# A graph layer on one core: q and k as two more columns of the value projection, denominators behind the weights

## The chip, the cores and the metric

One Trainium2 chip, one of its cores. The metric is device microseconds of one execution of the whole kernel, median of several runs. The kernel is written by hand: each engine has its own program, and engines wait for each other through semaphores.

## The reference

The input x is 32 batches of 512 channels by 1024 nodes, float32. What is computed per batch:

```
h = max(layernorm(x over the nodes), 0)
q = wq . h ; k = wk . h                     (one number per node)
scores[m, n] = leaky(q[n] + k[m])           (slope 0.01)
att = softmax(scores over n)
agg[c, m] = sum_n h[c, n] att[m, n]
out = x + max(adj . agg + bm, 0)            (adj is 512 x 512)
```

## The kernel before

The kernel multiplies the weights in first: v = h^T adj^T (1024 nodes by 512 outputs, `v_tile`), then out = v^T att (`unit`). Every product of two float32 operands is made of three f16 matmuls, hi.hi, hi.lo and lo.hi, so all tiles exist as an upper and a lower part (`h_hi`, `h_lo`, `v_hi`, `v_lo`, `p_hi`, `p_lo`).

**TensorE.** The work of one batch b is a period: eight units of 24 matmuls, each 512 columns wide (L385 to L387; units 0 to 3 are the first half of the output nodes, 4 to 7 the second), and then the v phase of batch b+2: eight node tiles of 12 matmuls, 512 columns (L362 to L364). In front of the v phase stands `project_qk`: 32 matmuls of 256 columns that fill the array four at a time with the small wq/wk tile (L325). Behind tile 1 stands `select_qk` (L334), which brings q and k to one column per node; behind tile 3 `spread_qmax` (L340). In unit 5 of each batch, ahead of node tile 2, stands `transpose_ab` (L347), which turns the scales of the next batch's softmax into rows. The accumulators are four PSUM banks `mix`, used in turn; a v tile takes one.

**The softmax.** leaky(q + k) splits: exp of it is the larger of two products of a row factor and a column factor. `exponentials` (ScalarE) makes the factors `cols` from `logs` (`q_head`, `q_tail` on VectorE). SyncE writes two of them to DRAM and loads them spread over all partitions as `den_row` (`write_den_rows`, `load_den_rows`). `denominator` (VectorE, L728) makes the row sums, 16 instructions a batch; `row_scales` (L735 to L739) their reciprocals. After `transpose_ab` and `copy_ab` (L685), SyncE writes and loads them as `ab_row`. The weights themselves are made in 16 steps a batch, eight for each half: `leak` (ScalarE, L491) into one of three PSUM banks `ring`, `weight` (VectorE, L749), `p_upper` (ScalarE, L499), `p_lower` (VectorE, L756).

**VectorE** runs `early(b)`: half 1 of batch b, whose eight weights are each followed by two denominators of batch b+1, then `row_scales`, two `h_lower`, `copy_ab`, two `h_lower`; and `late(b)`: half 0 of batch b+1, then the eight `v_lower` (L761) of batch b+2 with `q_rows`, `q_head`, `q_tail`, the `statistics` (L633) and the `normaliser` (L649 to L662, a chain of small dependent operations) of batch b+3 between them.

**ScalarE** runs in step: leak and p_upper, the normalised tiles `h_upper` (L465) and `h_full` (L471), `relu` of each unit (L512), `v_upper` (L503). **GpSimd** adds the residual to each unit (`finish`, L911). **SyncE** issues all transfers in one order: stores, residual loads, the ab rows, x of batch b+3, and at the end of the period the denominator rows of batch b+2.

Who waits for what around the change, as before has it:

```
            def transpose_ab(b):
                if at(b, first):
                    pe.wait_ge(s_az, 1)
                    pe.wait_ge(s_qc, Q_OPS + 4)
                pe.wait_ge(s_dn, cnt(b, D_OPS, D_OPS))
```

The first two batches are taken apart in a prologue of its own, written out by hand.

Of the kernel before, what the change touches and what calls it, by code (L numbers as in the profile page):

```python
# [25 lines left out]
F32 = mybir.dt.float32  # L26
F16 = mybir.dt.float16
# [16 lines left out]
def gnn_layer(nc, x, adj, wq, wk, bm, out):  # L44
# [7 lines left out]
    QG = 32  # L52
    NQ = P // QG
    QN = N // NQ
# [4 lines left out]
    with ExitStack() as ctx:  # L59
# [23 lines left out]
        wmT_hi = sb("wmT_hi", [P, CT, O], F16)  # L83
        wmT_lo = sb("wmT_lo", [P, CT, O], F16)
        wm_nat = sb("wm_nat", [P, OT, C])
        wqk = sb("wqk", [P, CT, QG], F16)
        select = sb("select", [P, NQ, 2])
        qk_rows = sb("qk_rows", [P, QN])
# [21 lines left out]
        ln_shift = sb("ln_shift", [P, 2, CT])  # L110
        qk = sb("qk", [P, 2, NT])
# [14 lines left out]
        mix = [bank(f"mix{i}") for i in range(MIX)]  # L126
# [3 lines left out]
        assert CT == 4 and NT == 8  # L130
        assert QN == 2 * P and NT == 2 * NQ
        rows_ps = small[:, 0:QN]
        ab_ps = small[:, 0:P]
        qk_ps = small[:, QN:QN + 2 * NT].rearrange("p (c g i) -> p c g i", c=2, i=2)
# [12 lines left out]
        s_wz = sem("wqk_zeroed")  # L147
        s_un = sem("unscales_ready")
        s_sel = sem("select_ready")
        s_wqk = sem("wqk_ready")  # L150
        s_wm = sem("wm_scaled")
# [8 lines left out]
        s_qk = sem("qk_done")  # L160
# [52 lines left out]
        def _(sp):  # L213
# [55 lines left out]
            write_den_rows(second)  # L269
            load_den_rows(second)  # L270

            def period(b, one, two, three):
                store(b, 0)
# [12 lines left out]
                if two:  # L286
                    write_den_rows(nxt(b, 2))
                    load_den_rows(nxt(b, 2))

# [14 lines left out]
        def _(pe):  # L304
            def transposed_weights():
                pe.wait_ge(s_id, 2)
                for ot in range(OT):
                    pe.wait_ge(s_wm, ot + 1)
# [6 lines left out]
            def project_qk(b):  # L315

                pe.wait_ge(s_hlo, cnt(b, CT, CT))
                if at(b, second):
                    pe.wait_ge(s_qc, 4)
                else:  # L320
                    wait(pe, s_at, cnt(b, 1, 0))
                for ct in range(CT):
                    for part, hp in enumerate((h_hi, h_lo)):
                        for g in range(NQ):
                            mm = pe.matmul(rows_ps[g * QG:(g + 1) * QG, :], wqk[:, ct, :],  # L325
                                           hp[:, b[1], ct, g * QN:(g + 1) * QN],
                                           start=(ct == 0 and part == 0), stop=(ct == CT - 1 and part == 1),
                                           tile_position=(0, g * QG))
                mm.then_inc(s_qk, 1)

            def select_qk(b):
                pe.wait_ge(s_qc, cnt(b, Q_OPS, 1))
                for c in range(2):
                    mm = pe.matmul(qk_ps[:, c, :, :], qk_rows[:, c * P:(c + 1) * P], select[:, :, :],  # L334
                                   start=True, stop=True)
                mm.then_inc(s_qk, 1)
# [5 lines left out]
            def transpose_ab(b):  # L342
                if at(b, first):
                    pe.wait_ge(s_az, 1)
                    pe.wait_ge(s_qc, Q_OPS + 4)
# [3 lines left out]
            def v_tile(b, nt):  # L349

                if nt < MIX and at(b, second):
                    pe.wait_ge(s_vlo[nt % 2], (nt + MIX) // 2 + 1)
                elif nt < MIX:
                    wait(pe, s_y[nt % 2], cnt(b, U // 2, (nt + MIX) // 2 + 1 - U))
                else:
                    pe.wait_ge(s_vlo[nt % 2], cnt(b, NT // 2, (nt - MIX) // 2 + 1))
                ps, nodes = mix[nt % MIX], slice(nt * P, (nt + 1) * P)
                for ct in range(CT):
                    if nt == 0 and at(b, first):
                        pe.wait_ge(s_wl, ct + 1)  # L360
# [585 lines left out]
```

## Time and profile before

| | us |
|---|---|
| median of 3 runs | 2088.57 |
| lowest and highest | 2087.33, 2088.61 |
| the profiled execution | 2090.47 |
| its span, first to last instruction | 2088.7 |
| TensorE busy (share of the span) | 2051.5 (98%) |
| VectorE busy | 1674.8 (80%) |
| ScalarE busy | 1221.5 (58%) |
| GpSimd busy | 379.6 (18%) |

Busy time counts an instruction from its start to its end; matmuls overlap, so their durations (379 ns for one of 512 columns) are longer than the step from one start to the next. The chain of waits that ended last lies on TensorE for 95% of the span.

### The profile page before, as it was taken

How to read it: one execution, taken by the hardware profiler on the slowest of the kernel's cores; microseconds unless marked ns; L12 is line 12 of the kernel's file. 1: busy time of each engine (PE TensorE's matmuls, PEld its weight loads, DVE VectorE, ACT ScalarE, POOL GpSimd, SP SyncE). 2: the span in 40 equal slices, each digit the busy share in tenths (PEclk: the TensorE clock that was granted, in tenths of full speed). 3: DMA queues.
4: the chain of work that ended last, by engine and by line, in shares of the span. 5: the costliest groups of instructions: out<-in, count | busy, mean ns of one | idle time of the engine just before them, and what ended most of it. 6: DMA issues, size and time to landing. Idle time of an engine off the chain costs nothing.

```text
span 2088.7 us, 33534 instructions
## 1 busy us (share of the span) xinstructions
PE 2051.5 (98%) x10448; PEld 950.3 (45%) x10448; DVE 1674.8 (80%) x3661; ACT 1221.5 (58%) x1871; POOL 379.6 (18%) x273
## 2 busy tenths in 40 slices
PE   5899999999999999999999999999999999999999
PEld 2344444444444444444444444444444444444444
DVE  7978878778887788887788877888877888778853
ACT  5556656556655566565566555665655665556634
POOL 1012211112111122111121111221111211112212
PEclk9999999999999999999999999999999999999999
DMA  5244433344324444333433234442334432343332
GB/s 195 64 155 142 148 99 123 138 160 141 133 84 136 151 141 146 104 118 137 161 141 133 84 136 151 141 146 105 117 137 161 141 131 86 136 152 141 106 101 76
DMA packets 126395, 271.46 MB, mean 130 GB/s; under 512 B 22624, under 2 KB 23136, under 8 KB 122208
## 3 DMA queue, kind: packets, MB, share of 16 engines
q1 hardware_dynamic: 123904, 269.01, 37.1%
q10 hardware_dynamic: 2400, 1.58, 0.3%
q14 instruction: 76, 0.62, 0.1%
q8 instruction: 15, 0.25, 0.1%
HBM read 202.91 MB, written 67.63 MB: 130 GB/s over the span
## 4 chain that ended last, share of the span: by engine, by line
PE 95%; DVE 3%; DMA 1%; POOL 0%; issue 0%; ACT 0%; POOLq 0%; SPq 0%; DVEq 0%
PE mix L385 21%; PE mix L387 21%; PE mix L386 21%; PE mix L362 10%; PE mix L363 10%; PE mix L364 10%; PE small L325 2%; DVE den_out L728 1%; PE small L334 1%; DMA xs<-in_x_dram 0%; DVE p_ring L749 0%; DVE p_lo L756 0%; DVE v_lo L761 0%; POOL wm_nat L893 0%; DMA den_row<-den_rows 0%
## 5 line engine op out<-in xcount | busy, mean ns | idle before, releaser
L385 PE MATMUL mix<-p_hi,v_hi 128*128 128x512 f16 x2048 | 776.3, 379 | 5.9 <-DVE p_lo L756 5.4
L386 PE MATMUL mix<-p_lo,v_hi 128*128 128x512 f16 x2048 | 776.2, 379 | 0.0
L387 PE MATMUL mix<-p_hi,v_lo 128*128 128x512 f16 x2048 | 776.2, 379 | 0.0
L911 POOL TENSOR_TENSOR res<-res,y 128x512 f32<-128x512 f32 x256 | 370.5, 1447 | 1688.2 <-ACT y L512 1688.2
L749 DVE SCALAR_TENSOR_TENSOR p_ring<-ab_row,cols,p_ring 128x512 f32<-128x512 f32 x512 | 377.1, 748 | 129.7 <-ACT p_ring L491 129.7
L491 ACT ACTIVATE p_ring<-ab_row,cols 128x512 f32<-128x512 f32 x512 | 349.5, 691 | 192.4 <-DMA ab_row<-ab_rows 132.3
L503 ACT ACTIVATE v_hi<-mix 128x512 f16<-128x512 f32 x256 | 152.7, 597 | 444.1 <-PE mix L364 443.5
L728 DVE SCALAR_TENSOR_TENSOR den_out<-den_row,cols 128x512 f32<-128x512 f32 x512 | 393.4, 806 | 1.0 <-DMA den_row<-den_rows 1.0
L362 PE MATMUL mix<-wmT_hi,h_hi 128*128 128x512 f16 x1024 | 389.1, 380 | 0.0
L364 PE MATMUL mix<-wmT_hi,h_lo 128*128 128x512 f16 x1024 | 388.8, 380 | 0.0
L363 PE MATMUL mix<-wmT_lo,h_hi 128*128 128x512 f16 x1024 | 388.8, 380 | 0.0
L756 DVE SCALAR_TENSOR_TENSOR p_lo<-p_ring,p_hi 128x512 f16<-128x512 f32 x512 | 351.6, 687 | 19.3 <-ACT p_hi L499 14.9
L499 ACT ACTIVATE p_hi<-p_ring 128x512 f16<-128x512 f32 x512 | 303.0, 592 | 67.8 <-DVE p_ring L749 67.5
L761 DVE SCALAR_TENSOR_TENSOR v_lo<-mix,v_hi 128x512 f16<-128x512 f32 x256 | 176.7, 691 | 195.6 <-ACT v_hi L503 191.7
L385 PEld LDWEIGHTS mix<-p_hi,v_hi 128*128 128x128 f16 x2048 | 200.3, 98 | 249.7 <-DVE p_lo L756 8.5
L387 PEld LDWEIGHTS mix<-p_hi,v_lo 128*128 128x128 f16 x2048 | 200.4, 98 | 241.6
L386 PEld LDWEIGHTS mix<-p_lo,v_hi 128*128 128x128 f16 x2048 | 200.4, 98 | 237.2
L512 ACT ACTIVATE y<-mix,bias_o,unscale_o 128x512 f32<-128x512 f32 x256 | 195.8, 765 | 29.2 <-PE mix L387 29.2
L471 ACT ACTIVATE h<-xs,ln_shift,ln_scale 128x1024 f32<-128x1024 f32 x120 | 145.0, 1232 | 107.3 <-DVE h_lo L691 107.3
L633 DVE BATCH_NORM_STATS2 stats<-xs 128x6 f32<-128x512 f32 x248 | 158.3, 680 | 8.6 <-DMA xs<-in_x_dram 8.6
L362 PEld LDWEIGHTS mix<-wmT_hi,h_hi 128*128 128x128 f16 x1024 | 103.0, 101 | 119.2 <-issue 5.9
L364 PEld LDWEIGHTS mix<-wmT_hi,h_lo 128*128 128x128 f16 x1024 | 100.3, 98 | 121.4 <-issue 1.0
(71 smaller groups left out, 838.9 us busy)
## 6 DMA issues: line engine op xcount, KB each, us to landing
res<-in_x_dram SPq DMA_DIRECT2D x256, 256.0 KB, 3.2
out_dram<-res SPq DMA_DIRECT2D x256, 256.0 KB, 2.1
xs<-in_x_dram SPq DMA_DIRECT2D x124, 512.0 KB, 6.5
den_row<-den_rows SPq DMA_DIRECT2D x32, 1024.0 KB, 4.6
ab_row<-ab_rows SPq DMA_DIRECT2D x64, 512.0 KB, 5.0
res<-in_x_dram SPq DMA_DIRECT2D x4, 512.0 KB, 5.0
wm_nat<-in_adj_dram ACTq DMA_DIRECT2D x1, 1024.0 KB, 12.2
den_rows<-cols SPq DMA_DIRECT2D x32, 8.0 KB, 1.6
```

The source lines that it names most:

```text
L362: pe.matmul(ps[:, :], hi, wmT_hi[:, ct, :], start=(ct == 0), stop=False)
L363: pe.matmul(ps[:, :], hi, wmT_lo[:, ct, :], start=False, stop=False)
L364: mm = pe.matmul(ps[:, :], lo, wmT_hi[:, ct, :], start=False, stop=(ct == CT - 1))
L385: pe.matmul(ps[:, :], v_hi[:, b[1], nt, chans], p_hi[:, hf, nt, :], start=(nt == 0), stop=False)
L386: pe.matmul(ps[:, :], v_hi[:, b[1], nt, chans], p_lo[:, hf, nt, :], start=False, stop=False)
L387: mm = pe.matmul(ps[:, :], v_lo[:, b[1], nt, chans], p_hi[:, hf, nt, :], start=False, stop=(nt == NT - 1))
L491: act.activation(ring[t % RING][:, :], ab_row[:, 1, hf * HALF:(hf + 1) * HALF], ACT.Copy, scale=cols[:, b[1], 1, nt:nt + 1]).then_inc(s_lk, 1)
L499: act.activation(p_hi[:, hf, nt, :], ring[t % RING][:, :], ACT.Copy, scale=P_SCALE).then_inc(s_phi, 1)
L728: dve.scalar_tensor_tensor(out=den_out[:, nodes], in0=den_row[:, 0, nodes], scalar=cols[:, b[1], 2, nt:nt + 1], in1=den_row[:, 1, nodes], ...
L749: dve.scalar_tensor_tensor(out=ring[t % RING][:, :], in0=ab_row[:, 0, hf * HALF:(hf + 1) * HALF], scalar=cols[:, b[1], 0, nt:nt + 1], in1= ...
L756: dve.scalar_tensor_tensor(out=p_lo[:, hf, nt, :], in0=ring[t % RING][:, :], scalar=P_SCALE, in1=p_hi[:, hf, nt, :], op0=ALU.mult, op1=ALU ...
L911: pool.tensor_tensor(res[:, k, :], res[:, k, :], y[:, k % 2, :], ALU.add).then_inc(s_add, 1)
```

## The change

q and k are no longer projected apart. The tiles `wmT_hi` and `wmT_lo` are cut into two halves of 256 outputs, and the first half has two more columns, wq and wk. A v tile takes two PSUM banks (`pair`), half a bank each, and each of its 12 matmuls of 512 columns becomes one of 258 and one of 256. So there are two v tiles' worth of accumulators in place of four, and a tile waits for the split of the tile two before it. ScalarE copies the two columns out ahead of `v_hi`, as `qk4`. `project_qk` and `select_qk` go, but the first batch keeps a projection of its own of 96 matmuls with two columns.

`q_head` of batch b+1 moves to the start of `early(b)`, `q_tail` behind the third p_lo of half 1, `exponentials` behind the fourth p_hi, and SyncE's denominator rows to the start of its period. All 16 denominators stand behind the weights of half 1. `transpose_ab` stands ahead of node tile 0 of unit 5, `spread_qmax` in unit 0 ahead of node tile 6. On ScalarE the normalised tiles move behind half 1, between the relus; relu 7 moves into half 0. The normaliser moves from behind v_lower 6 to behind v_lower 5.

```diff
             def v_tile(b, nt):
+                if nt == 0:
+                    pe.wait_ge(s_hlo, cnt(b, CT, CT))
...
-                ps, nodes = mix[nt % MIX], slice(nt * P, (nt + 1) * P)
+                    pe.wait_ge(s_vlo[nt % 2], cnt(b, NT // 2, nt // 2))
+                ps, nodes = pair[nt % 2], slice(nt * P, (nt + 1) * P)
...
-                    pe.matmul(ps[:, :], hi, wmT_hi[:, ct, :], start=(ct == 0), stop=False)
-                    pe.matmul(ps[:, :], hi, wmT_lo[:, ct, :], start=False, stop=False)
-                    mm = pe.matmul(ps[:, :], lo, wmT_hi[:, ct, :], start=False, stop=(ct == CT - 1))
+                    for half, cols_of in enumerate((OH + QK, OH)):
+                        pe.matmul(ps[:, half, 0:cols_of], hi, wmT_hi[:, ct, half, 0:cols_of],
+                                  start=(ct == 0), stop=False)
+                    for half, cols_of in enumerate((OH + QK, OH)):
+                        pe.matmul(ps[:, half, 0:cols_of], hi, wmT_lo[:, ct, half, 0:cols_of], start=False, stop=False)
+                    for half, cols_of in enumerate((OH + QK, OH)):
+                        mm = pe.matmul(ps[:, half, 0:cols_of], lo, wmT_hi[:, ct, half, 0:cols_of],
+                                       start=False, stop=(ct == CT - 1))
                 mm.then_inc(s_v, 1)
...
                 for nt in range(NT):
-                    if one and k == MIX + 1 and nt == 2:
+                    if one and k == MIX + 1 and nt == 0:
                         transpose_ab(nxt(b))
+                    if one and (k, nt) == ((1, 2) if at(b, first) else (0, 6)):
+                        spread_qmax(nxt(b))
...
             def early(b, one, two):
                 h = nxt(b, 2)
+                if one:
+                    q_head(nxt(b))
                 weight(b, NT)
                 for nt in range(NT):
                     if nt < NT - 1:
                         weight(b, NT + nt + 1)
-                    if one:
+                    p_lower(b, NT + nt)
+                    if one and nt == 2:
+                        q_tail(nxt(b))
+                if one:
+                    for nt in range(NT):
                         denominator(nxt(b), nt)
-                    p_lower(b, NT + nt)
-                if one:
                     row_scales(nxt(b))
...
@@ ScalarE, period @@
-                    if two and nt in (0, 3, 7):
-                        h_upper(h, (0, 3, 7).index(nt))
-                    if two and nt in (1, 5):
-                        h_full(h, nt // 4)
-                    if nt in (2, 4, 6):
-                        relu(b, nt // 2 - 1)
+                    if one and nt == 3:
+                        exponentials(nxt(b))
+                    if nt == 5:
+                        relu(b, 0)
                 if two:
+                    h_upper(h, 0)
+                    h_full(h, 0)
+                relu(b, 1)
+                if two:
+                    h_upper(h, 1)
+                    h_full(h, 1)
+                relu(b, 2)
+                if two:
+                    h_upper(h, 2)
                     h_upper(h, 3)
                 relu(b, 3)
```

The prologue changes too: VectorE scales half of the projection weights, GpSimd the other half and wq and wk, and the hand-written orders of both are new.

How the instructions move, VectorE, `early` of one batch, from the last step but one of half 1 to the first transfer's source (L749 is `weight`, L728 `denominator`, L756 `p_lower`, L735 to L739 `row_scales`, L691 `h_lower`, L685 `copy_ab`); before:

```order
L749 SCALAR_TENSOR_TENSOR p_ring<-ab_row,cols,p_ring 128x512
L728 SCALAR_TENSOR_TENSOR den_out,den_part<-den_row,cols 128x512 x2
L756 SCALAR_TENSOR_TENSOR p_lo<-p_ring,p_hi 128x512
L728 SCALAR_TENSOR_TENSOR den_out,den_part<-den_row,cols 128x512 x2
L756 SCALAR_TENSOR_TENSOR p_lo<-p_ring,p_hi 128x512
L735 TENSOR_TENSOR den<-den_part 128x8
L737 RECIPROCAL ab_pad<-den 128x8
L739 TENSOR_TENSOR ab_pad<-cols,ab_pad 128x8
L691 TENSOR_TENSOR h_lo<-h,h_hi 128x1024 x2
L685 COPY ab_t<-small 16x128
```

and in the changed kernel (L729 weight, L736 p_lower, L708 denominator, L715 to L719 row_scales, L670 h_lower, L664 copy_ab):

```order
L729 SCALAR_TENSOR_TENSOR p_ring<-ab_row,cols,p_ring 128x512
L736 SCALAR_TENSOR_TENSOR p_lo<-p_ring,p_hi 128x512 x2
L708 SCALAR_TENSOR_TENSOR den_out,den_part<-den_row,cols 128x512 x16
L715 TENSOR_TENSOR den<-den_part 128x8
L717 RECIPROCAL ab_pad<-den 128x8
L719 TENSOR_TENSOR ab_pad<-cols,ab_pad 128x8
L670 TENSOR_TENSOR h_lo<-h,h_hi 128x1024 x2
L664 COPY ab_t<-small 16x128
```

The denominators are now 16 in one run.

SyncE, the denominator rows and the stores around them; before (L237 and L241 are the denominator rows out and in, L232 a store, L228 a residual load; the period of the first batch begins with the first store below, and the rows ahead of it are the second batch's):

```order
L252 DMA ab_row<-ab_rows 128x2x512 x2
L237 DMA den_rows<-cols 128x2x8
L241 DMA den_row<-den_rows 128x2048
L232 DMA out_dram<-res 128x512 x2
L228 DMA res<-in_x_dram 128x512
```

and in the changed kernel, from the end of the first period into the second:

```order
L224 DMA res<-in_x_dram 128x512 x2
L233 DMA den_rows<-cols 128x2x8
L237 DMA den_row<-den_rows 128x2048
L228 DMA out_dram<-res 128x512 x2
L224 DMA res<-in_x_dram 128x512
```

The transfers L233 and L237 read alike, but in the changed kernel they are of the next batch, whose exponentials are made in half 1 of this period; before they were of the batch after the next, made in the v phase.

## Rows read from the trace of the kernel before

**Rows 1.** the page: busy time of TensorE (PE), its weight loads (PEld) and the others.

```profile
PE 2051.5 (98%) x10448; PEld 950.3 (45%) x10448; DVE 1674.8 (80%) x3661; ACT 1221.5 (58%) x1871; POOL 379.6 (18%) x273
```

**Rows 2.** timeline of TensorE, one period: start us, us, engine, line, instruction.

```profile
979.53 0.38 PE L385 MATMUL mix<-p_hi,v_hi 128*128 128x512 f16 x1
...
1006.72 0.27 PE L347 MATMUL small<-ident,ab_pad 128*128 128x128 f32 x1
1006.83 0.38 PE L385 MATMUL mix<-p_hi,v_hi 128*128 128x512 f16 x1
...
1020.86 0.38 PE L387 MATMUL mix<-p_hi,v_lo 128*128 128x512 f16 x1
...
1022.16 0.39 PE L362 MATMUL mix<-wmT_hi,h_hi 128*128 128x512 f16 x1
...
1027.13 0.38 PE L364 MATMUL mix<-wmT_hi,h_lo 128*128 128x512 f16 x1
...
1027.71 0.38 PE L362 MATMUL mix<-wmT_hi,h_hi 128*128 128x512 f16 x1
```

**Rows 3.** timeline of VectorE (DVE), same period.

```profile
978.39 0.20 DVE L649 BATCH_NORM_AGGREGATE moments<-stats 128x2 f32<-128x12 f32 x1
...
981.32 0.69 DVE L761 SCALAR_TENSOR_TENSOR v_lo<-mix,v_hi 128x512 f16<-128x512 f32 x1
...
998.85 1.76 DVE L728 SCALAR_TENSOR_TENSOR den_out<-den_row,cols 128x512 f32<-128x512 f32 x1
...
1000.54 0.74 DVE L728 SCALAR_TENSOR_TENSOR den_out<-den_row,cols 128x512 f32<-128x512 f32 x1
...
1001.21 0.68 DVE L756 SCALAR_TENSOR_TENSOR p_lo<-p_ring,p_hi 128x512 f16<-128x512 f32 x1
...
1003.76 0.62 DVE L735 TENSOR_TENSOR den<-den_part 128x8 f32<-128x8 f32 x1
...
1004.82 2.36 DVE L691 TENSOR_TENSOR h_lo<-h,h_hi 128x1024 f16<-128x1024 f32 x2
...
1013.67 1.42 DVE L749 SCALAR_TENSOR_TENSOR p_ring<-ab_row,cols,p_ring 128x512 f32<-128x512 f32 x2 [3.88 <-ACT p_ring L491]
...
1024.63 0.41 DVE L700 COPY qk_rows<-small 128x256 f32<-128x256 f32 x1
1025.59 0.69 DVE L761 SCALAR_TENSOR_TENSOR v_lo<-mix,v_hi 128x512 f16<-128x512 f32 x1 [0.55 <-ACT v_hi L503]
...
1034.33 0.28 DVE L712 TENSOR_REDUCE qmax<-small 128x1 f32<-128x128 f32 x1
...
1035.05 1.28 DVE L633 BATCH_NORM_STATS2 stats<-xs 128x6 f32<-128x512 f32 x2
```

**Rows 4.** timeline of ScalarE (ACT), the first exponential.

```profile
1036.28 0.21 ACT L480 ACTIVATE cols<-logs 128x16 f32<-128x16 f32 x1
```

**Rows 5.** timeline of SyncE's queue, the load of the denominator rows.

```profile
1038.09 0.33 SPq L241 DMA_DIRECT2D den_row<-den_rows  x1
```

**Rows 6.** that load (L241), all 32 of them, from issue to landing.

```profile
DMA to landing us min/median/max: 4.2/4.6/5.3
```

**Rows 7.** timeline of GpSimd (POOL), same period.

```profile
994.64 1.55 POOL L911 TENSOR_TENSOR res<-res,y 128x512 f32<-128x512 f32 x1 [3.65 <-ACT y L512]
998.79 1.27 POOL L911 TENSOR_TENSOR res<-res,y 128x512 f32<-128x512 f32 x1 [2.60 <-ACT y L512]
1002.64 1.71 POOL L911 TENSOR_TENSOR res<-res,y 128x512 f32<-128x512 f32 x1 [2.58 <-ACT y L512]
```

**Rows 8.** the page's costliest groups: ScalarE's relu and full tile, busy, mean ns.

```profile
L512 ACT ACTIVATE y<-mix,bias_o,unscale_o 128x512 f32<-128x512 f32 x256 | 195.8, 765 | 29.2 <-PE mix L387 29.2
L471 ACT ACTIVATE h<-xs,ln_shift,ln_scale 128x1024 f32<-128x1024 f32 x120 | 145.0, 1232 | 107.3 <-DVE h_lo L691 107.3
```

**Rows 9.** timeline of TensorE, prologue, the first v tile.

```profile
30.40 0.59 PE L362 MATMUL mix<-wmT_hi,h_hi 128*128 128x512 f16 x1
```

**Rows 10.** timeline of VectorE, prologue, the first weight.

```profile
75.81 1.42 DVE L749 SCALAR_TENSOR_TENSOR p_ring<-ab_row,cols,p_ring 128x512 f32<-128x512 f32 x2 [0.76 <-ACT p_ring L491]
```

More of the change, by code:

```diff
@@ L123, in gnn_layer @@
         ab_dram = nc.dram_tensor("ab_rows", (2, NT, P), F32, kind="Internal").ap()
-        mix = [bank(f"mix{i}") for i in range(MIX)]
+        pair = [ctx.enter_context(nc.psum_tensor(f"pair{i}", [P, 2, 512], F32)) for i in range(2)]
+        mix = [pair[i // 2][:, i % 2, :] for i in range(MIX)]
         ring = [bank(f"p_ring{i}") for i in range(RING)]
@@ L313, in transposed_weights, with project_first_qk @@
                             mm.then_inc(s_wt, 1)
[L315 to L335, printed above, removed]
+            def project_first_qk():
+                pe.wait_ge(s_wqk, 2)
+                pe.wait_ge(s_hlo, CT)
+                for nt in range(NT):
+                    for ct in range(CT):
+                        nodes = slice(nt * P, (nt + 1) * P)
+                        hi, lo = h_hi[:, 0, ct, nodes], h_lo[:, 0, ct, nodes]
+                        w_hi, w_lo = wmT_hi[:, ct, 0, OH:], wmT_lo[:, ct, 0, OH:]
+                        pe.matmul(qk_ps[:, nt, :], hi, w_hi, start=(ct == 0), stop=False)
+                        pe.matmul(qk_ps[:, nt, :], hi, w_lo, start=False, stop=False)
+                        mm = pe.matmul(qk_ps[:, nt, :], lo, w_hi, start=False, stop=(ct == CT - 1))
                 mm.then_inc(s_qk, 1)
@@ L502, in v_upper @@
                 act.wait_ge(s_v, cnt(b, NT, nt + 1))
[L503 removed]
+                ps = pair[nt % 2]
+                if not at(b, first):
+                    act.activation(qk4[:, nt, :], ps[:, 0, OH:OH + QK], ACT.Copy)
+                act.activation(v_hi[:, b[1], nt, :].rearrange("p (h o) -> p h o", h=2), ps[:, :, 0:OH], ACT.Copy,
                                scale=1.0 / H_SCALE).then_inc(s_vhi, 1)
@@ L575, in _ @@
             v_upper(second, 2)
-            exponentials(second)
             v_upper(second, 3)
@@ L835, in _ @@
             denominator(first, 0)
-            for ct in range(CT):
-                h_lower(second, ct)
-                v_lower(first, 3 + ct)
-                denominator(first, 1 + ct)
+            h_lower(second, 0)
+            v_lower(first, 3)
+            denominator(first, 1)
+            h_lower(second, 1)
+            v_lower(first, 4)
+            h_lower(second, 2)
+            v_lower(first, 5)
+            denominator(first, 2)
+            h_lower(second, 3)
+            v_lower(first, 6)
+            denominator(first, 3)
             v_lower(first, 7)
-            q_rows(second)
+            denominator(first, 4)
             denominator(first, 5)
+            v_lower(second, 0)
             denominator(first, 6)
-            q_head(second)
             denominator(first, 7)
             row_scales(first)
-            q_tail(second)
-            v_lower(second, 0)
             v_lower(second, 1)
```

185 lines of the change are left out of this document (73 added, 112 removed).

## The prediction

> **What bounds the kernel now.** I read the page's busy times first. TensorE is busy 98% of the span, and it has as many weight loads as matmuls [rows 1], so the second use of one stationary tile loads it again. Then I read one period of TensorE's timeline, from the first matmul of a batch's unit 0 at 979.53, which I call time zero; times written +x below are us from there [rows 2]. From 1006.83 to 1020.86 are 65 matmuls of 512 columns with no hole, 0.2158 us each: 213.3 ns of columns at the upper clock level of 2.4 GHz, and 2.5 ns beside them. The period is 288 of these (62.16), two transposes of 0.11, and the q and k part: from the last matmul before it to the first tile is 1.30, less one step 1.08; the select is 0.58 less 0.2158, so 0.36 [rows 2]. Sum 63.8. Nothing waits: everything else is cover. Next I read VectorE (DVE), because it decides when TensorE could be made to wait. Its reciprocal chain ends at 1004.82, which is +25.3, and TensorE asks for it at 1006.72, which is +27.2 [rows 2, 3]. That margin of 1.9 us is the number to watch.
>
> **What comes off TensorE.** 1.08 + 0.36 = 1.44 us a period. Spread and transpose stay.
>
> **What goes on.** Every 512-column matmul becomes 258 and 256 columns. By columns at 2.4 GHz and 2.5 ns each, that is 110.0 + 109.2 = 219.2 ns for 215.8. Times 96 it is +0.32 us a period. Lower bound 0.08 (only the two columns more). Upper bound: if a load were not covered by a matmul half as long, it costs about what the select's load and 8-column matmul cost, 0.36/4 = 0.09 us each, 17 us a period. I take the low value, as a 128x128 f16 load already lies under the transpose, whose step is 0.11 [rows 2]. The Trainium skill (TensorE: Matmul & The Clock Gate, LDWEIGHTS) gives columns / 1.2 ns for a load, 107 ns here, so it would be covered with 2 ns to spare; no run here shows such loads in a row. Net on TensorE: -1.1 us a period, 30 periods with a v phase, -33 us.
>
> **The two-bank tiles.** A tile may now start only when the tile two before it is split, where it was four. v_lo starts 0.84 after a tile's end (1022.16 + 12 x 0.2158 = 1024.75, then 1025.59) and takes 0.69 [rows 2, 3]. The qk4 copy adds 0.1 to 0.2 on ScalarE (a small operation there is 0.21 [rows 4]). Done 1.7 after the tile's end, wanted after 2.63: covered. The normaliser, 2.93 us (978.39 to 981.32 [rows 3]), now stands before v_lower 6; from tile 5's end: 0.95 + 0.61 + 2.93 + 0.69 = 5.2, and unit 0 wants it at 5.26. Just covered; I count 0 and keep 0.2 a period as the other end.
>
> **The denominators, moved.** This is the term that decides. They were laced between the weights of half 1, two behind each weight; now all 16 stand behind the last p_lo, and the transpose that needs their result is asked for two node tiles earlier, behind five units: 5 x 24 x 0.2158 + 0.11 = +26.0. VectorE by its new order:
> - v_lower 7 from +0.95 to +1.56; q_head, three small operations, 0.5 (four take 0.72, 1034.33 to 1035.05 [rows 3]): +2.06.
> - Half 1 without denominators runs as half 0 does now, 10.96 (1013.67 to 1024.63 [rows 3]), with q_tail's 0.72 in it: +13.7.
> - q_tail ends after weights 8 to 11 and p_lo 8 to 10, about 5.5 in: +7.7, exponentials at +8.0. From the exponentials (1036.28 + 0.21) to the issue of the row load is 1.6, and landing is 4.6, 4.2 to 5.3 [rows 4 to 6]: the denominator rows arrive at +14.2. SP stands free: their write is now the first thing in its period. So the denominators start at +14.2, not +13.7. SP's store of unit 0 is queued behind that write, but is due only near +12.
> - 16 denominators at 0.67 (1000.54 to 1001.21 [rows 3]): 10.8, to +25.0.
> - GpSimd. One denominator took 1.76 where its neighbour takes 0.74: the step from 998.85 to 1000.54 is 1.69, 1.01 too much, and GpSimd's residual addition had begun at 998.79 and ran 1.27 [rows 3, 7]. Both read two SBUF tensors. The reverse is there too: the addition at 994.64 took 1.55, and the one at 1002.64 took 1.71 and then held VectorE's tiny add at 1003.76 for 0.62 [rows 3, 7]. With the laced order one or two additions a period cost VectorE something; the others fell on weights and p_lo, which read one operand from PSUM. Now the run of denominators is unbroken from +14 on, and ScalarE puts its relus between the normalised tiles, 1.23 each with 0.1 of overlap, relu 0.77 [rows 8]: p_hi 15 ends at +13, two h tiles, relu 1 at +16, two h tiles, relu 2 at +19, two h tiles, relu 3 (unit 3 is done at +21) at +22. Each starts an addition. All three fall into the run: 3 x 1.01 = 3.0, to +28.0.
> - Row scales: 0.53, being 1.06 (1003.76 to 1004.82) less the hold [rows 3]: +28.6. TensorE needs 0.15 to start again.
>
> TensorE thus stands from +26.0 to +28.7, **2.7 us in each of 31 periods**, +84 us. It is not given back later: VectorE takes up the next period only from that period's own tile 7.
>
> The Trainium skill (SBUF — State Buffer, Who interferes with whom) says the port pair shared by VectorE and GpSimd is an exclusive lock that the first to issue holds for its whole instruction; the rows agree. By that rule an addition that has waited on one denominator goes ahead of the next, and the sum is the one above; without it the rows leave the stall between 0 and 2.7 us, which is 2061 to 2145.
>
> **What is late next.** From the row scales the two h_lo, the copy, the two transfers and the leak take 8.85 (1004.82 to 1013.67), half 0 10.96, v_lower 0 0.69 [rows 3]: 20.5 after. TensorE wants it after 15.8 for three units and 5.3 for two tiles, 21.1. Covered by 0.6, a third relu between half 0's steps perhaps 0.3 of it.
>
> **Prologue.** TensorE's tile 0 starts at 30.40 now [rows 9]. The weights get their scale sooner, but 96 loads with matmuls of 2 columns stand before it. Bounds for one: 0.18 (the select's 0.09 at half the clock) down to nearly zero; I take 0.07, as f16 should load faster than the select's f32, 7 us from about 25.5, tile 0 at 32.5. VectorE then has the second batch's statistics ahead of v_lower 0, and with two buffers TensorE waits for it, about 1 us at tiles 2, 3, 5 and more at the second batch's tile 5, where v_lower 3 stands behind the copy of the transposed scales. Followed through, the first weight moves from 75.81 [rows 10] to about 80.3: +4.5, ends 0 and +12.
>
> **Sum.** Span 2088.7 - 33 + 84 + 4.5 = 2144. The profiled execution lasted 1.8 longer than its span, and the median of the runs is 1.9 below it: forecast 2144, say 2145.
>
> **Rivals.**
> 1. *The lock goes the other way, or the order hides it: faster.* If VectorE keeps its turn between denominators, the additions wait and nobody needs them soon. The chain ends at +25.6, before +26.0, and there is no stall: 2145 - 84 = 2061. The point from which it decides: (33 - 4.5) / 31 = 0.9 us; a stall shorter than that leaves the kernel faster. For it: no row shows an addition waiting inside a longer run. Against: 994.64 + 1.55 - 1.27 = 994.92, the moment when the denominator before it had read its data; GpSimd is quick enough. Chance 0.15.
> 2. *Fewer holds.* Two additions in the run give 2114, one 2083, if relus fall elsewhere. 0.08.
> 3. *The clock falls in the stall.* The first tile's matmuls run at the lower level after the idle prologue; a stall of near 3 us in each period is new, and no row shows what it does. If each cost some 2 us at half speed, +60: 2205. The Trainium skill (TensorE: Matmul & The Clock Gate, HAM oscillation) says that gaps between bursts of matmuls can bring the lower clock back. 0.05.
> 4. *Uncovered weight loads.* 0.09 x 192 a period, far above 2500. 0.01.
> 5. *A later row load* (landing at its 5.3 and more, behind other traffic [rows 6]): a stall of 3.3 to 4.2 us, 2163 to 2190. 0.06.
>
> **Numbers.** The forecast itself, with a stall of 2.0 to 3.3 us, has 0.65: 2122 to 2163 and a few us of prologue. The range 2080 to 2190 adds rivals 2 and 5 and leaves out 1, 3 and 4. About 0.2%, 4 us, is what a measurement can tell from no change. Faster 0.18 (rival 1 and one hold), same 0.04, slower 0.78.
>
> **What would show it.** TensorE idle before the transpose of ab_pad, 2.7 us in 31 periods, released by the reciprocal chain; 16 denominators in a row, three of them at about 1.75 us; denominator rows landing near +14; v tile steps of 0.110 us; q and k gone from TensorE. If that idle time is under 1 us, or no more than one denominator in a run is held, I am wrong.

## The result, and the profile after

The changed kernel takes 2173.39 us (median of 6 runs, 2169.66 to 2177.21), the kernel before beside it 2088.59. The ratio is 1.0403, 95% interval 1.0389 to 1.0418: the change makes the kernel 4% slower. The forecast was 2145 with a range of 2080 to 2190. The profiled execution took 2175.07, its span 2173.3.

The page's busy times, which answer to [rows 1]:

```profile
PE 2060.8 (95%) x12464; PEld 1213.7 (56%) x12464; DVE 1728.7 (80%) x3628; ACT 1236.8 (57%) x2119; POOL 372.0 (17%) x271
```

TensorE's share fell from 98% to 95%. The waits of TensorE say where (engine line waited for: us in total, times, longest us):

```profile
PE small L330 <- DVE ab_pad L719: 73.0, 31, 4.4
...
PE pair L350 <- DVE v_lo L741: 10.6, 5, 5.8
...
PE pair L350 <- ACT y L497: 2.4, 9, 0.4
```

The first is the forecast stall, in 31 periods, ahead of the transpose of `ab_pad`. TensorE's timeline of one period (start us, us, engine, line, instruction, idle before it), which answers to [rows 2]:

```profile
999.25 0.38 PE L350 MATMUL pair<-wmT_hi,h_hi 128*128 128x258 f16 x2
...
1017.20 0.39 PE L350 MATMUL pair<-wmT_hi,h_hi 128*128 128x258 f16 x2
...
1017.91 0.39 PE L379 MATMUL pair<-p_hi,v_hi 128*128 128x512 f16 x1
...
1043.71 0.38 PE L381 MATMUL pair<-p_hi,v_lo 128*128 128x512 f16 x1
1046.50 0.33 PE L330 MATMUL small<-ident,ab_pad 128*128 128x128 f32 x1 [2.40 <-DVE ab_pad L719]
1046.66 0.38 PE L379 MATMUL pair<-p_hi,v_hi 128*128 128x512 f16 x1
...
1048.00 0.63 PE L379 MATMUL pair<-p_hi,v_hi 128*128 128x512 f16 x1
1048.43 0.63 PE L380 MATMUL pair<-p_lo,v_hi 128*128 128x512 f16 x1
```

Time zero of this period is 1017.91. TensorE asks at +26.0 and gets the transpose at +28.6. A stall is counted here from start to start, less one ordinary step; that is 0.16 more than the idle time in the brackets of a row, which counts from the modelled end of the matmul before. From 999.25 to 1017.20 are 81 pairs of 258 and 256 columns, 0.2216 us a pair. And from 1048.00 on a matmul of 512 columns takes 0.43 us where it took 0.216: the clock is at its lower level. Two stretches of about the same length behind two stalls show it (us, busy times of PE, PEld, DVE, ACT and POOL, PEclk, DMA share, GB/s):

```profile
1047.80:1051.00 3.20, 3.20 (x10) 1.12 (x9) 3.15 (x4) 2.95 (x3) 0.17 (x1) 0.52 0.01 3
1115.00:1118.00 3.00, 3.00 (x16) 1.34 (x15) 2.95 (x4) 2.71 (x3) 0.21 (x1) 1.00 0.01 3
```

PEclk is 0.52 behind the one stall, that is 1.2 GHz, and 1.00 behind the next. VectorE's timeline of the same period, which answers to [rows 3]:

```profile
1031.84 0.75 DVE L708 SCALAR_TENSOR_TENSOR den_out<-den_row,cols 128x512 f32<-128x512 f32 x1 [0.80 <-DMA den_row<-den_rows]
...
1033.86 1.75 DVE L708 SCALAR_TENSOR_TENSOR den_out<-den_row,cols 128x512 f32<-128x512 f32 x1
...
1036.22 1.85 DVE L708 SCALAR_TENSOR_TENSOR den_out<-den_row,cols 128x512 f32<-128x512 f32 x1
...
1040.01 1.75 DVE L708 SCALAR_TENSOR_TENSOR den_out<-den_row,cols 128x512 f32<-128x512 f32 x1
...
1046.28 0.17 DVE L719 TENSOR_TENSOR ab_pad<-cols,ab_pad 128x8 f32<-128x8 f32 x1
1046.45 2.36 DVE L670 TENSOR_TENSOR h_lo<-h,h_hi 128x1024 f16<-128x1024 f32 x2
```

and GpSimd's, which answers to [rows 7]:

```profile
1033.38 1.68 POOL L892 TENSOR_TENSOR res<-res,y 128x512 f32<-128x512 f32 x1 [2.85 <-ACT y L497]
1036.24 1.27 POOL L892 TENSOR_TENSOR res<-res,y 128x512 f32<-128x512 f32 x1 [1.18 <-ACT y L497]
1039.87 1.34 POOL L892 TENSOR_TENSOR res<-res,y 128x512 f32<-128x512 f32 x1 [2.36 <-ACT y L497]
```

Three additions meet three held denominators, about 1 us each, and the row scales end at +28.5. It is so in every period: each of the 31 runs of 16 has exactly three denominators of 1.74 to 1.85 and 13 under 0.8, where the kernel before has one held denominator in each of 30 batches.

**Where the time went.** A period was 63.83; the mean of 29 steady ones is now 66.38. Its parts: 63.83, less 1.44 for q and k, plus 0.57 for the pairs (96 x (0.2216 - 0.2158)), plus 2.39 of stall, plus 0.76 of matmuls at the lower clock (13 periods with 1.7 us each), plus 0.15 of short waits at v tiles: 66.26. The 0.12 that is left lies in small differences between steps and is not placed. Over 30 periods the mean gives +76; the rest lies in the first period, the last and the prologue.

### The profile page after: what moved, and what is told of

It reads as the page before. It is cut to its first block, busy times and chain, and to the rows that moved or that the text cites. A ratio compares the mean times of both kernels' runs of the same rounds, so it can differ in the third digit from the quotient of the medians.

```text
span 2173.3 us, 37744 instructions
## 1 busy us (share of the span) xinstructions
PE 2060.8 (95%) x12464; PEld 1213.7 (56%) x12464; DVE 1728.7 (80%) x3628; ACT 1236.8 (57%) x2119; POOL 372.0 (17%) x271
## 4 chain that ended last, share of the span: by engine, by line
PE 47%; DVE 17%; issue 17%; DMA 12%; ACT 6%; POOL 0%; DVEq 0%; ACTq 0%; POOLq 0%; SPq 0%
PE pair L350 10%; PE pair L355 10%; PE pair L353 9%; DVE den_out L708 7%; DMA den_row<-den_rows 7%; PE pair L379 6%; PE pair L381 6%; PE pair L380 6%; DVE p_ring L729 3%; ACT p_ring L472 2%; DMA den_rows<-cols 2%; DVE p_lo L736 2%; DMA ab_row<-ab_rows 2%; ACT v_hi L488 1%; ACT y L497 1%
## 5 line engine op out<-in xcount | busy, mean ns | idle before, releaser
L379 PE MATMUL pair<-p_hi,v_hi 128*128 128x512 f16 x2048 | 787.2, 384 | 0.0
L381 PE MATMUL pair<-p_hi,v_lo 128*128 128x512 f16 x2048 | 786.1, 384 | 0.0
L380 PE MATMUL pair<-p_lo,v_hi 128*128 128x512 f16 x2048 | 785.8, 384 | 0.0
L729 DVE SCALAR_TENSOR_TENSOR p_ring<-ab_row,cols,p_ring 128x512 f32<-128x512 f32 x512 | 376.3, 746 | 128.0 <-ACT p_ring L472 128.0
L708 DVE SCALAR_TENSOR_TENSOR den_out<-den_row,cols 128x512 f32<-128x512 f32 x512 | 442.1, 928 | 26.4 <-DMA den_row<-den_rows 26.4
L350 PE MATMUL pair<-wmT_hi,h_hi 128*128 128x258 f16 (+1 forms) x2048 | 394.6, 274 | 13.3 <-DVE v_lo L741 10.6
L353 PE MATMUL pair<-wmT_lo,h_hi 128*128 128x258 f16 (+1 forms) x2048 | 392.5, 273 | 0.0
L355 PE MATMUL pair<-wmT_hi,h_lo 128*128 128x258 f16 (+1 forms) x2048 | 392.3, 273 | 0.0
L736 DVE SCALAR_TENSOR_TENSOR p_lo<-p_ring,p_hi 128x512 f16<-128x512 f32 x512 | 347.0, 686 | 28.7 <-ACT p_hi L480 22.7
L381 PEld LDWEIGHTS pair<-p_hi,v_lo 128*128 128x128 f16 x2048 | 202.6, 99 | 248.3 <-issue 12.0
L379 PEld LDWEIGHTS pair<-p_hi,v_hi 128*128 128x128 f16 x2048 | 203.9, 100 | 244.5 <-issue 15.8
L380 PEld LDWEIGHTS pair<-p_lo,v_hi 128*128 128x128 f16 x2048 | 202.6, 99 | 237.7 <-issue 11.2
L497 ACT ACTIVATE y<-pair,bias_o,unscale_o 128x512 f32<-128x512 f32 x256 | 198.3, 774 | 55.7 <-PE pair L381 55.5
L353 PEld LDWEIGHTS pair<-wmT_lo,h_hi 128*128 128x128 f16 x2048 | 199.1, 97 | 29.0
L355 PEld LDWEIGHTS pair<-wmT_hi,h_lo 128*128 128x128 f16 x2048 | 198.5, 97 | 28.6
## 6 DMA issues: line engine op xcount, KB each, us to landing
wm_nat<-in_adj_dram ACTq DMA_DIRECT2D x1, 1024.0 KB, 12.1
```

Source lines behind the costliest of these rows:

```text
L350: pe.matmul(ps[:, half, 0:cols_of], hi, wmT_hi[:, ct, half, 0:cols_of], start=(ct == 0), stop=False)
L353: pe.matmul(ps[:, half, 0:cols_of], hi, wmT_lo[:, ct, half, 0:cols_of], start=False, stop=False)
L355: mm = pe.matmul(ps[:, half, 0:cols_of], lo, wmT_hi[:, ct, half, 0:cols_of], start=False, stop=(ct == CT - 1))
L379: pe.matmul(ps[:, :], v_hi[:, b[1], nt, chans], p_hi[:, hf, nt, :], start=(nt == 0), stop=False)
L380: pe.matmul(ps[:, :], v_hi[:, b[1], nt, chans], p_lo[:, hf, nt, :], start=False, stop=False)
L381: mm = pe.matmul(ps[:, :], v_lo[:, b[1], nt, chans], p_hi[:, hf, nt, :], start=False, stop=(nt == NT - 1))
```

## Experiments

Each was timed in three rounds; times are medians, ratios are against the kernel before, run beside it. "Tile wait" is TensorE's wait ahead of a v tile, counted as the stall is. The kernel before gave 2088 to 2090 each time.

### 1. Additions behind the denominators

```diff
             def finish(b, k):
+                if k == 1 and not at(b, last):
+                    pool.wait_ge(s_dn, cnt(nxt(b), D_OPS, D_OPS))
                 pool.wait_ge(s_xr[k], cnt(b, 16, 16))
```

> The changed kernel, but GpSimd holds back the residual additions of units 1 to 3 until the denominators and row scales of the next batch are done. Theory A (the three holds of the denominators make the stall): no denominator over 0.8 us, the row scales end 3.0 us earlier, near +25.5, TensorE no longer idle before the transpose of ab_pad (under 0.3 us a period against 2.4), the clock stays up, and the time falls by the stall and the slow stretches, 77 + 25 us, to about 2071 us; up to 2100 if the held additions now fall on the h_lo subtractions behind the row scales and delay the ab rows. Theory B (the late denominator rows and the length of the run decide, holds or not): stall still over 1.5 us, time above 2130 us.

It took 2332.54 us, 1.1165 (1.1146 to 1.1183) of the kernel before. The holds are gone: every denominator takes 0.74 to 0.75, the row scales end at +25.3, and the stall at the transpose is gone. That part of the theory stands. But the time went up by 159. Timelines of GpSimd, then of SyncE's queue:

```profile
1043.19 8.94 POOL L894 TENSOR_TENSOR res<-res,y 128x512 f32<-128x512 f32 x4 [12.78 <-DVE ab_pad L719]
```

```profile
1045.49 0.34 SPq L228 DMA_DIRECT2D out_dram<-res  x1
...
1050.88 0.45 SPq L242 DMA_DIRECT2D ab_rows<-ab_t  x1
1053.53 0.89 SPq L248 DMA_DIRECT2D ab_row<-ab_rows  x2
```

SyncE's transfer of the scales stands behind the stores, and the stores wait for the additions: it goes out at 1050.88, 7.8 us behind the row scales (1043.1) where it is 2.6 in the changed kernel (1049.03 for 1046.45), so half 0 is late. ScalarE's relu 3 waits for its buffer up to 12.1 us. TensorE then waits 162.3 us in 60 places for relus, and the lower clock comes with it, about 80 us in 29 periods. I had not counted the way through SyncE's row. (How much of the 159 is due to it alone is not shown; experiment 8 moves it together with the copy.)

### 2 and 4. The transpose asked for later

```diff
-                    if one and k == MIX + 1 and nt == 0:
+                    if one and k == MIX + 1 and nt == 5:
```

(and nt == 2 in the fourth.)

> The changed kernel with the transpose of ab_pad five node tiles later in unit 5, 3.2 us. Theory A (VectorE's chain through the ab rows and half 0 to v_lower 0 is as late as the transpose): no idle time before the transpose, but 2.0 to 2.5 us a period of it at v tiles 1 and 2, where pair tiles wait for relu 7 and for v_lower 0; in two short pieces the clock may stay up, 2148 us, or 2173 if it falls. Theory B (only the place of the transpose asks too early): the idle time goes and nothing takes its place, 2071 to 2080 us.

> The changed kernel with the transpose of ab_pad ahead of node tile 2 of unit 5, where the kernel before has it, 1.3 us later. Theory A: idle time before the transpose 1.1 to 1.3 us in place of 2.4, and about 1.1 us new at v tile 2, since v_lower 0 is not earlier; sum unchanged, but no gap long enough for the clock: 2145 to 2150 us. Theory B: idle time halves with nothing new: 2105 to 2115 us. If the clock still falls as often, 25 us more on either.

Node tile 5: 2163.67, 1.0366 (1.0349 to 1.0383). Node tile 2: 2146.80, 1.0272 (1.0251 to 1.0293). Waits of TensorE, node tile 5, then node tile 2:

```profile
PE pair L350 <- ACT y L497: 69.8, 30, 3.3
```

```profile
PE pair L350 <- ACT y L497: 37.9, 29, 1.8
PE small L330 <- DVE ab_pad L719: 31.3, 31, 3.5
```

The stall moves from the transpose to v tile 1 and nearly keeps its size: 2.5 us a period in one piece, or 1.0 and 1.4 in two. So the late chain reaches the v tiles anyway; there was no slack behind the transpose. In two pieces the clock nearly always stays up: it falls in 1 of 29 periods and costs 2 us, against 13 falls and 22 us in the changed kernel and 11 falls and 19 us with one piece at the tile. That is the 17 us between the two kernels.

### 3. The kernel before, with its denominators in one run

The 16 denominators behind the weights of half 1, with the changed kernel's order on ScalarE, in the kernel before; nothing else.

> The kernel before, with only the 16 denominators in one run behind the weights of half 1 and ScalarE's order of the changed kernel in half 1 (relus 0 to 3 and the normalised tiles); q and k, four banks and the transpose ahead of node tile 2 as before. Theory A: the run starts near +13, as the rows are there since the v phase, three holds, row scales end near +27.3, and TensorE asks at +27.2: stall 0.1 to 0.4 us a period, clock up, 2090 to 2102 us. Theory B (a run of 16 is dear wherever it stands): stall over 2 us, above 2150 us.

It took 2097.29 us, 1.0042 (1.0028 to 1.0056). The clock stays up and the stall is at most 0.24 in a steady period. The denominators' mean is 925 ns, as in the changed kernel (928; 806 before), with three held ones in each run: the run with its holds alone costs little, 9 us, as long as half 1 holds no q_tail and waits for no row, and the transpose is asked for two node tiles later. It is the combination that makes the stall.

### 5. Narrow additions

```diff
-                pool.tensor_tensor(res[:, k, :], res[:, k, :], y[:, k % 2, :], ALU.add).then_inc(s_add, 1)
+                pool.tensor_tensor(res[:, k, 0:8], res[:, k, 0:8], y[:, k % 2, 0:8], ALU.add).then_inc(s_add, 1)
```

The layer's part is thus added in 8 columns of each 512; the output lacks it in the other 504.

> The changed kernel, but each residual addition of GpSimd covers 8 of its 512 columns; the other columns keep x alone, so the output lacks the layer's part there. All waits and orders stay. Theory A (GpSimd's full additions hold three denominators by 1.0 us each): no denominator over 0.9 us, row scales end near +25.4 instead of +28.5, no idle time before the transpose of ab_pad, which TensorE reaches at +26.0, and no wait at v tile 2; clock up; 2068 to 2078 us. Theory B (the late rows and the length of the run make the stall): stall still over 1.5 us, above 2120 us.

It took 2074.00 us, 0.9931 (0.9914 to 0.9947), as expected: faster than the kernel before. The denominators in the changed kernel, then in this one (count, busy us in total, mean ns, idle time before them):

```profile
L708 DVE SCALAR_TENSOR_TENSOR den_out<-den_row,cols 128x512 f32<-128x512 f32 x512 | 442.1, 928 | 26.4 <-DMA den_row<-den_rows 26.4
```

```profile
L708 DVE SCALAR_TENSOR_TENSOR den_out<-den_row,cols 128x512 f32<-128x512 f32 x512 | 347.5, 746 | 31.7 <-DMA den_row<-den_rows 31.7
```

The mean falls to 746 ns, none is over 0.8 us, and the stall at the transpose is gone, in an otherwise unchanged program. So the holds by GpSimd's additions make the stall, and the lower clock with it. The edit also shortens every other addition, so what it gives back is the price of all of them. The periods take 63.0 to 63.7.

### 6 and 7. The copy of the scales first, and earlier exponentials

```diff
                     row_scales(nxt(b))
+                    copy_ab(nxt(b))
                 if two:
                     h_lower(h, 0)
                     h_lower(h, 1)
-                if one:
-                    copy_ab(nxt(b))
-                if two:
                     h_lower(h, 2)
                     h_lower(h, 3)
```

The transpose stands ahead of node tile 4 in both. In the seventh `q_tail` also stands behind the first p_lo, `exponentials` behind the second p_hi of half 1 and `spread_qmax` ahead of node tile 4 of unit 0.

> The changed kernel with the transpose of ab_pad ahead of node tile 4 of unit 5 (+28.6), and on VectorE copy_ab directly behind the row scales, ahead of the two h_lo subtractions. Theory A (two deadlines of one chain: the transpose, and through the ab rows half 0 and v_lower 0 at v tile 2): the holds stay, row scales end at +28.5, so the transpose hardly waits (under 0.2 us), and the chain behind it is about 2 us shorter, so v tile 2 waits under 0.5 us; clock up; 2070 to 2085 us, faster than the kernel before. Theory B (the chain behind is not shortened by the copy's place, since the rows or relu 7 come last): 1.5 us or more a period at v tiles 1 or 2, above 2115 us.

> As e6, and q_tail behind the first p_lo of half 1 instead of the third, spread_qmax ahead of node tile 4 of unit 0, the exponentials behind the second p_hi. Theory A: the denominator rows land before the weights end, the run starts 0.8 us earlier near +13.1, row scales end near +27.7; nothing waits at the transpose or at v tile 2; 2068 to 2075 us, at most 5 us under e6. Theory B (TensorE now waits for q_head in unit 0): idle time before the transpose of qmax_p, slower than e6.

They took 2119.48 us, 1.0147 (1.0131 to 1.0164), and 2117.62, 1.0137 (1.0120 to 1.0154): better than the change by 54 and 56, but not the 2070 to 2085 and 2068 to 2075 expected. The copy no longer stands behind two h_lo, the stall at the transpose is gone, and a wait at v tile 1 stays, alternating from the fifth steady period on: in the seventh kernel 0.8 to 1.0 in one period and 2.2 to 2.6 in the next. Waits of TensorE in the sixth:

```profile
PE pair L350 <- ACT y L497: 39.2, 30, 2.4
```

### 8. Additions held back, with SyncE's row in order

The edit of the first, the copy first, and the transfers of the scales in SyncE's row of unit 1 in place of unit 4.

> As e1 (additions of units 1 to 3 held back behind the row scales), with copy_ab directly behind the row scales and SyncE's ab rows ahead of the store of unit 1 instead of unit 4. Theory A (e1 lost its time because SyncE's ab rows stood behind stores that waited for the held additions, and because the copy stood behind two held h_lo): no hold, row scales near +25.5, ab rows issued near +26.6, no wait at v tiles, 2068 to 2085 us. Theory B (what cost e1 its time is ScalarE, whose relu 3 waits for an addition and keeps half 0 back): still over 2150 us.

It took 2113.21 us, 1.0121 (1.0103 to 1.0138), and not the 2068 to 2085 expected. Every period but 12 takes 62.9 to 63.1 with no wait at all. The 12 are every second one from the fifth steady period on; they take 65.6 to 67.6 with one tile wait of 2.5 to 3.0, and those over 67 have a fall of the clock besides. So the parts are right, and something comes in every second period only.

### 9 and 10. ScalarE's last relus earlier

```diff
-                        if nt == 3:
+                        if nt == 1:
                             relu(b, 6)
-                        if nt == 5:
+                        if nt == 3:
                             relu(b, 7)
```

The ninth is the seventh kernel with this edit, the tenth the eighth.

> This is the kernel of 2117.6 (transpose ahead of node tile 4, the scales' copy ahead of the h_lo, early exponentials), with ScalarE's relu 6 of half 0 behind its second p_hi in place of the fourth, and relu 7 behind its fourth in place of the sixth. Theory B (the v tiles waited for relu 7 alone, 0.5 to 1.0 us in one period and 2.2 in the next, because it stood late in half 0): both waits go, the clock stays at the upper level, the period is what the additions without weight showed, about 63.0, and the whole 2066 to 2080. Rival C (v_lower 0 is just as late: half 0's steps on VectorE end it, and the relus moved ahead make half 0 later still): a wait of 0.5 to 1.5 us stays at v tile 1 or 2, now released by VectorE, 2090 to 2115.

> This is the kernel of 2113.2 (the additions of units 1 on wait for the denominators, the scales' copy ahead of the h_lo, SyncE's two transfers of the scales early in its row of unit 1), with relus 6 and 7 moved as in the other kernel. It had periods of 63.0 with no wait and others of 65.9 to 67.5 with a wait for the relu at v tile 1 or 2. Theory B: relu 7 comes late in those because it stands late; moved, all periods become 63.0 to 63.5 and the whole 2066 to 2085. Rival C: relu 7 there is late because it waits for the buffer of addition 5, which waited behind held-back additions; moving it in ScalarE's order then only stops p_hi behind it, and the time stays at 2105 to 2125.

They took 2120.53 us, 1.0155 (1.0138 to 1.0172), and 2120.55, 1.0150 (1.0133 to 1.0167): 3 and 7 us worse than without. Waits of TensorE in the ninth:

```profile
PE pair L350 <- DVE v_lo L741: 52.0, 36, 5.8
```

The wait has about the same size in the steady periods, 2.3 in those that had 2.2 to 2.6. It stands one tile later (v tile 2) and is now released by VectorE, as rival C has it. I had taken relu 7 for the cause because it was named as releaser. That was a misreading: half 0 itself began late.

### 11. VectorE's loop written out

I went back to VectorE's timeline of the eighth kernel, in a fast period and then in a slow one (start us, us, instruction, idle before it):

```profile
560.59 7.84 DVE L670 TENSOR_TENSOR h_lo<-h,h_hi 128x1024 f16<-128x1024 f32 x4
...
568.35 1.40 DVE L729 SCALAR_TENSOR_TENSOR p_ring<-ab_row,cols,p_ring 128x512 f32<-128x512 f32 x2
...
629.21 1.23 DVE L670 TENSOR_TENSOR h_lo<-h,h_hi 128x1024 f16<-128x1024 f32 x1 [0.24 <-ACT h L452]
634.54 1.42 DVE L729 SCALAR_TENSOR_TENSOR p_ring<-ab_row,cols,p_ring 128x512 f32<-128x512 f32 x2 [4.11 <-issue]
```

In the fast period the first weight follows the last h_lo at once. In the slow one VectorE stands 4.11 us for nothing that the profile names. Its loop body is two batches long, and in the program its jump back stands exactly between that h_lo and that weight:

```diff
-            with dve.Fori(1, PAIRS - 1) as i:
+            for i in range(1, PAIRS - 1):
                 late((i, 0), True, True, True)
                 early((i, 1), True, True)
                 late((i, 1), True, True, True)
                 early((i + 1, 0), True, True)
```

> This is the kernel of 2113.2 (additions held back behind the denominators, the scales' copy and SyncE's two transfers first) with VectorE's hardware loop written out: the same instructions in the same order, no jump. In the kernel of 2113.2 VectorE stood 2.8 to 4.2 us in every second period ahead of the first weight of half 0, released by nothing that the profile shows, 12 times, 39.9 us in all; this is exactly the place where its loop jumps back, and it is in exactly those periods that TensorE waited 2.5 to 3.0 us at a v tile; the other periods took 62.98 with no wait. Theory J (the jump, with the fetch of instructions behind it, costs 3 to 4 us and decides): the idle time released by nothing goes, all periods are 63.0 to 63.3, the whole 2065 to 2075, faster than the kernel before. Rival K (the stall is something else at that place, such as the row load's landing or the additions' hold on the h_lo, and the profile names it badly): 2105 to 2115, as it was. Rival L (straight code must be fetched too, and the fetches fall elsewhere): stalls without releaser at other places, 2080 to 2105.

**2066.97** (2064.99 to 2068.96), 0.9898 (0.9882 to 0.9915): 1.0% faster than the kernel before, 46 less than the eighth. All 29 steady periods take 62.93 to 63.16, with next to no wait left in them. The page's busy times, and its queue of instruction transfers, first of this kernel, then that queue of the eighth:

```profile
PE 2028.6 (98%) x12464; PEld 1212.2 (59%) x12464; DVE 1722.5 (83%) x3628; ACT 1239.2 (60%) x2119; POOL 398.0 (19%) x271
...
q14 instruction: 37, 0.30, 0.0%
```

```profile
q14 instruction: 76, 0.62, 0.1%
```

39 transfers of instructions are gone, three for each of the loop's 13 rounds.

The packets of that queue in the eighth kernel's trace say more. VectorE's idle time without releaser comes 12 times, 2.78 to 4.22 us long, and in each of the 12 one transfer of 8 KB of instructions starts in it, 0.7 to 2.2 us after VectorE fell idle. The first weight starts 1.76 to 1.80 us behind the end of that transfer, whether the idle time is the shortest or the longest. So VectorE waits for these instructions, and how late their transfer starts sets how long. With the loop written out transfers go on, 28 of them between 280 and 2000 us, and VectorE waits for none: rival L did not come.

### 12. The same, additions not held back

> This is the kernel of 2117.6 (the transpose ahead of node tile 4, the scales' copy first, early exponentials, additions not held back) with VectorE's hardware loop written out. It had waits at the v tile of 0.8 to 1.0 us in every second period and of 2.2 to 2.5 in those in which the loop jumps back. Theory J (the difference between the two kinds is the jump): every period has the short wait, 63.8 to 64.0 against 62.95 with the additions held back, the clock stays up, and the whole is 2067 + 30 x 0.95 = 2095, 2085 to 2100. That leaves the three holds of the denominators by GpSimd as what the rest is. Rival K (the two kinds of period come from the two buffers of a batch pair, such as the transfers of x, not from the jump): 2112 to 2120, with the two kinds as before. If relu 7's place alone were left, the wait is named ScalarE's; if half 0's, VectorE's.

It took 2095.49 us, 1.0029 (1.0018 to 1.0041), as worked out. Waits of TensorE:

```profile
PE pair L350 <- ACT y L497: 23.7, 30, 1.0
```

All periods have the short wait now, 63.7 to 64.2. The jump was worth 22 us here and 46 with the additions held back. I take the 28 between this kernel and the eleventh for the holds of the denominators, for the most part. That is argued and not shown, as the two also differ in the place of the transpose, in q_tail, the spread and the exponentials, and in SyncE's row.

## Why the prediction was right, and where it was off

**The mechanism held.** The stall stands where it was put, in 31 periods, released by the reciprocal chain. The working step by step: half 1 ended at +13.1 (forecast +13.7); the denominators began at +13.9, released by their DMA (+14.2); three additions held three of them (1.75, 1.85, 1.75 against a forecast of 1.76); row scales at +28.5 (+28.6); TensorE asked at +26.0 (+26.0). The stall itself was 2.39 in the mean for 2.7. The holds are not what varies: from the first denominator to the last it is 13.86 to 14.07 in all steady periods. What varies is the start of the run, +13.4 to +14.3, +13.8 in the mean for the forecast +14.2, and the stall goes with it. That an addition which has waited on one denominator goes ahead of the next held in all 31 runs, against rivals 1 and 2. Experiment 5 shows the price of GpSimd's additions as a whole: 2173.39 less 2074.00, 99 us. The Trainium skill (SBUF — State Buffer, Who interferes with whom) calls the port pair an exclusive lock; the trace agrees, with 1.0 us for each of three holds.

**The step that failed: rival 3, "the clock falls in the stall", as a case of 0.05 beside the forecast, +60 if it came.** It came in 13 of 29 steady periods, at 1.7 us each, 22 us, and once more in the last one before the end. That is the largest term in the 28 between 2145 and 2173. The price per fall (about 2 us forecast) was nearly right, the chance was not, and it should have stood in the sum as a part, not as a case of all or nothing. What decides in which period it falls is open: stalls of 2.34 to 2.88 were followed by the lower level and stalls of 1.93 to 2.69 were not. The Trainium skill (TensorE: Matmul & The Clock Gate, HAM oscillation) warns that gaps between bursts of matmuls bring the lower clock back. The trace agrees, at a PEclk of 0.52 behind 1048.

**What was luck.** 2173 lies above the 2122 to 2163 that a stall of 2.0 to 3.3 us was to give. It lies inside 2080 to 2190, but the upper end of that range had been set for a later row load (rival 5) and left the falling clock out. That the range holds the result is luck as far as the clock goes; the stall and its cause were foreseen.

**What goes on TensorE.** "219.2 ns for 215.8" was too low: a pair takes 221.6, so +0.57 a period for +0.32, 7 us in all. The 514 columns are 214.2 ns of it at 2.4 GHz, so 3.7 ns lie beside those of each matmul, not 2.5. Rival 4, uncovered loads at 0.09 us each, did not come: there are 12464 loads, and the pairs show no step of that length. The net gain of 0.87 a period is confirmed by experiment 11, whose 62.96 is 0.87 below 63.83.

**The two-bank tiles, and "what is late next", covered by 0.6, perhaps 0.3.** Right in size: waits of 0.3 to 0.55 in 10 of 29 periods, 4 us in all. They stand at v tile 1, released by relu 7, which ScalarE issues inside half 0, not by v_lower 0 as I had it; no later tile waits, so the normaliser is covered. But it is this chain that kept experiments 2, 4, 6 and 7 from their gain, and it held a term that I had not seen: the jump of VectorE's loop. In the kernel before and in the change a transfer of instructions also starts where the loop jumps back (at 1009.65 and 1051.29), and both hide it under VectorE's wait for the leak (3.88 [rows 3] and 4.24). An estimate from the 1.8 us that VectorE took behind the end of such a transfer: it could have gone on at 1011.9 and 1054.0, and the leak let it go at 1013.67 and 1055.66.

**Prologue.** Off in its parts, near in its sum. The 96 loads with two columns take 0.027 each, not 0.07, and tile 0 starts at 27.68, not at 32.5; in the old kernel it was 30.40 [rows 9]. The first weight is at 75.00, not 80.3 [rows 10]. But TensorE then waits 5.80 at a tile of the second batch, the stall of the first period is 4.16, and the second transpose comes at 115.55 for 113.08: +2.5 for +4.5.

**The sum,** by the transposes of `ab_pad` in the two traces. Up to the second, 115.55 for 113.08: +2.5. From there to the last, 30 periods, 1994.2 for 1914.9: +79.3. The forecast for these is 30 x (2.7 - 1.1) = 48. Of the 31 above it the falls of the clock are 24, the pairs 7, the waits at v tiles 4, the last stall (4.59) 2 and the steps not placed 3; the shorter stalls take 9 back. Behind the last transpose it is 63.5 for 60.7: +2.8. Together +84.6, span against span, where the forecast had +55.5. So the other misses cancel for the most part, and what is left is about the size of the clock's term.

## What to carry to other kernels

When a run of two-operand VectorE work on SBUF lies on the critical chain, count each GpSimd addition that falls into it at what it holds (here 1.0 us, for an addition of 1.27), and look for who else stands behind the addition before you hold it back: on ScalarE for the buffer, on the DMA queue for the store. A stall of 2 to 3 us in TensorE can cost more than itself, since the clock fell behind nearly half of them here; two short ones were cheaper than one long one, by 17 us. And when a loss comes in every second period, look where the hardware loop jumps: the page of the profile names such a wait "issue", and a loop's jump is best put where its engine waits anyway, as it was in the kernel before.

## What the runs showed of the hardware that I had not expected

- A jump back of VectorE's hardware loop costs it up to 4.2 us (2.8 to 4.2 in 12 rounds of experiment 8, seen behind the end of the last instruction), and goes when the loop is written out. 39 transfers of instructions go with it. In all 12 rounds VectorE goes on 1.76 to 1.80 us behind the end of one such transfer, so the time is that of fetching the instructions behind the jump. Why the transfer starts 0.7 us after VectorE fell idle in one round and 2.2 in another is open.
- 96 matmuls of 2 columns with their loads take 0.027 us each in the prologue:

```profile
25.20 0.17 PE L317 MATMUL small<-wmT_hi,h_hi 128*128 128x2 f16 x1
25.22 0.17 PE L318 MATMUL small<-wmT_lo,h_hi 128*128 128x2 f16 x1
```

  The load of a stationary tile of 128x128 in f16 can thus follow another at a quarter of the 107 ns quoted in the prediction, though the record of each of these loads is itself 104 to 108 ns long: they overlap. The Trainium skill (TensorE: Matmul & The Clock Gate, Weight-path perf modes) describes a fast weight load that is on for 128 weights of a type other than FP32, which fits.
- The same stall length was followed by the lower clock in some periods and not in others, mostly by turns.
